# A six-layer transformer stretch on one core: ScalarE writes the first attention's mask, and three stages get their first operands sooner

## What is computed

```python
scores = jnp.einsum('bqhe,bkhe->bhqk', Q, K) / np.sqrt(d_head).astype(np.float32)
scores = jnp.where(causal, jnp.float32(IGNORE), scores)
A = jax.nn.softmax(scores, axis=-1)
```

## Time and profile before, and how to read them

| | |
|---|---|
| three runs | 1570.81, 1572.22, 1576.1 us; median 1572.22 |
| the profiled execution | 1575.96 us, its span in the trace 1574.0 us |
| TensorE matmul busy | 1528.8 us, 97% |
| TensorE weight load busy | 1319.7 us, 84% |
| VectorE busy | 992.5 us, 63% |
| ScalarE busy | 692.1 us, 44% |
| GpSimd busy | 204.5 us, 13% |
| mean granted TensorE clock | 0.989 of full |

### The profile page before, as it was taken

How to read it: one execution, slowest core, us unless ns; L and a number is a source line. 1 busy time by engine, 2 the same in 40 slices (tenths; PEclk the granted TensorE clock), 3 DMA queues, 4 the chain that set the end, 5 groups by cost and what they waited for, 6 DMA issues and landing times.

```text
span 1574.0 us, 28636 instructions
## 1 busy us (share of the span) xinstructions
PE 1528.8 (97%) x11080; PEld 1319.7 (84%) x11080; DVE 992.5 (63%) x2131; ACT 692.1 (44%) x1812; POOL 204.5 (13%) x215
## 2 busy tenths in 40 slices
PE   7999999999999999999999899999988999999997
PEld 6888888789999999988888767777766989999996
DVE  6777777875454545575666567788876464454547
ACT  3544444532222222223233267788875444444443
POOL 1322222310000000011000024121221300000001
PEclk9999999999999999999999989999999999999999
DMA  6000000001010101000000466678850000000101
GB/s 216 1 2 15 8 35 1 28 27 39 27 40 27 52 27 39 23 11 34 1 34 1 53 102 86 87 101 127 111 89 28 1 27 28 28 27 17 36 0 53
DMA packets 43082, 66.51 MB, mean 42 GB/s; under 512 B 4577, under 2 KB 33505, under 8 KB 42849
## 3 DMA queue, kind: packets, MB, share of 16 engines
q1 hardware_dynamic: 42976, 65.09, 20.3%
HBM read 36.24 MB, written 2.10 MB: 24 GB/s over the span
## 4 chain that ended last, share of the span: by engine, by line
PE 90%; DVE 5%; ACT 1%; DMA 1%; issue 1%; SPq 1%; POOL 0%; DVEq 0%; POOLq 0%; ACTq 0%
PE ps L85 24%; PE ps L86 23%; PE ps L87 22%; PE ps L1823 3%; PE ps L1837 2%; PE ps L392 2%; PE ps L403 2%; PE ps L416 2%; PE ps L1813 2%; PE ps L1868 2%; PE ps L1851 1%; PE ps L1810 1%; DMA nQs<-nQc_h 1%; PE ps L384 1%; SPq L1648 1%
## 5 line engine op out<-in xcount | busy, mean ns | idle before, releaser
L843 ACT ACTIVATE m2hT_h<-ps 128x512 fp32r<-128x512 f32 x128 | 76.7, 599 | 281.4 <-PE ps L87 281.4
L967 DVE TENSOR_TENSOR m6hT_l<-m6h,m6hT_h 128x512 fp32r<-128x512 f32 x128 | 88.6, 692 | 169.8 <-ACT m6hT_h L841 169.8
L969 DVE SCALAR_TENSOR_TENSOR m2hT_l<-ps,m2hT_h 128x512 fp32r<-128x512 f32 x128 | 88.5, 691 | 163.4 <-ACT m2hT_h L843 163.4
L840 ACT ACTIVATE m6h<-ps,m6b 128x512 f32<-128x512 f32 x128 | 88.2, 689 | 197.7 <-PE ps L87 193.8
L1949 ACT ACTIVATE nPr<-ps,negm 128x128 f32<-128x128 f32 x512 | 147.2, 384 | 27.3 <-DVE negm L2050 26.8
L87 PE MATMUL ps<-w_h,m6hT_l 128*128 128x256 f32 x512 | 144.4, 282 | 0.0
L85 PE MATMUL ps<-w_h,m6hT_h 128*128 128x256 f32 x512 | 143.5, 280 | 0.6 <-DVE m6hT_l L967 0.6
L86 PE MATMUL ps<-w_l,m6hT_h 128*128 128x256 f32 x512 | 143.7, 281 | 0.0
L87 PE MATMUL ps<-m2w_h,m2hT_l 128*128 128x256 f32 x448 | 126.8, 283 | 0.0
L86 PE MATMUL ps<-m2w_l,m2hT_h 128*128 128x256 f32 x448 | 126.7, 283 | 0.0
L85 PE MATMUL ps<-m2w_h,m2hT_h 128*128 128x256 f32 x448 | 126.3, 282 | 0.0
(11 more groups left out here) (318 smaller groups left out, 4327.2 us busy)
## 6 DMA issues: line engine op xcount, KB each, us to landing
nKm<-nKc_h SPq DMA_DIRECT2D x64, 128.0 KB, 4.3
nQs<-nQc_h SPq DMA_DIRECT2D x64, 128.0 KB, 5.9
raw<-in_w_e1i SPq DMA_DIRECT2D x9, 512.0 KB, 3.2
raw<-in_w_e1o SPq DMA_DIRECT2D x9, 512.0 KB, 3.2
raw<-in_w_e6i SPq DMA_DIRECT2D x9, 512.0 KB, 3.4
raw<-in_w_e6o SPq DMA_DIRECT2D x9, 512.0 KB, 3.3
nKm<-nKc_l SPq DMA_DIRECT2D x32, 128.0 KB, 4.8
nQs<-nQc_l SPq DMA_DIRECT2D x32, 128.0 KB, 5.9
```

Source lines behind the costliest of these rows:

```text
L840: nc.scalar.activation(c.h32[:, u % 2, :], ps[:, u % 2, :], ACT.Gelu, bias=bias)
L843: nc.scalar.activation(c.hT[0][:, ch, :], ps[:, u % 2, :], ACT.Relu).then_inc(c.s["hi_ready"], 1)
L967: last = nc.vector.tensor_tensor(c.hT[1][:, ch, :], c.h32[:, u % 2, :], c.hT[0][:, ch, :].bitcast(F32), ALU.subtract)
L969: last = nc.vector.scalar_tensor_tensor(c.hT[1][:, ch, :], ps[:, u % 2, :], 0.0, c.hT[0][:, ch, :].bitcast(F32), ALU.max, ALU.subtract)
```

## The change

ScalarE copies the bf16 mask from SBUF into each score bank when the exponentials of that bank are done (semaphore `masked`), for steps 1 to 31; the mask matmuls stay in step 0 alone, and Q K is added to the bank with `start=False`. In the first mixture the two x transposes of the routed stage stand ahead of `down(-2)`, and DVE does their low halves before group 2's normalisation and the last combine, which move behind the router's logits. In the last group of the routed stage x stands at chunk 6, the keys around `up(8)`, the queries after chunk 9's spread and `down(7)`. The last residual is done between the value copies, its statistics at n = 2 and its normalisation at n = 4; POOL's `residual(0)` waits for that. The keys of group 0 lie in `raw`, so layer 5's weights are loaded by `load_e6`, after the key layouts of group 0 have been read. The last mixture's x of group 0 has a place of its own (in wA5, dead by then), so only the third x waits for the layouts; its items are at other quads.

```diff
@@ scores (tensor)
-            if p > 0:
-                pe.wait_ge(s["p_exp"], 2 * p)
-            for half in range(2):
-                nc.tensor.matmul(ps[:, WSB[half], :], identb[:, :], causal[:, :, :].rearrange("p a b -> p (a b)"),
-                                 start=True, stop=False)
+                for half in range(2):
+                    nc.tensor.matmul(ps[:, WSB[half], :], identb[:, :], causal[:, :, :].rearrange("p a b -> p (a b)"),
+                                     start=True, stop=False)
+            else:
+                pe.wait_ge(s["masked"], 2 * p)
...
-                                            W.KT[G % 2][rows64, 4 * u + i, tok], start=False, stop=i == QH - 1)
+                                            W.KT[G % 2][rows64, 4 * u + i, tok], start=False, stop=p > 0 or i == QH - 1,
+                                            skip_group_check=p > 0)
@@ w_scalar
+        def mask(half):
+
+            nc.scalar.activation(ps[:, WSB[half], :], causal[:, :, :].rearrange("p a b -> p (a b)"),
+                                 ACT.Identity).then_inc(s["masked"], 1)
...
                     exponentials(2 * p + half)
+                if p < NP - 1:
+                    act.wait_ge(s["p_exp"], 2 * p + half + 1)
+                    mask(half)
@@ mix_setup
-        c.XT = pair(m, tag + "XT", [P, NG, DC, GT])
+        own = pair(m, tag + "XT", [P, NG, DC, GT])
+        c.XT = [[x[:, g, :, :] for g in range(NG)] for x in own]
...
+            for x, x0 in zip(c.XT, pair(Region(nc, a5_at, 8 * KB), tag + "XT0", [P, DC, GT])):
+                x[0] = x0[:, :, :]
@@ mix_tensor_parts
-                pe.wait_ge(N.s["z_ready"], NSEQS - GB)
-            if c.gelu and k == 4:
+                pe.wait_ge(N.s["z_ready"], NSEQS - GB - 1)
+            if c.gelu and k == 2:
+                pe.wait_ge(c.s["lt_taken"], 1)
+            elif c.gelu and k == 4:
...
-            pe.wait_ge(c.s["g_evac"], max(g + 1, 2) * DC + 2)
+            pe.wait_ge(c.s["g_evac"], (g + 1) * DC + 2)
@@ mix_tensor
-        down(i, -2)
         if between:
             between()
+        down(i, -2)
         down(i, -1, halves=c.gelu)
@@ mix_vector
                 if between and u == NU - 1:
                     between(0)
-                normalise(q - NG)
+                    between(1)
+                else:
+                    normalise(q - NG)
             weights(i, u)
         if not c.gelu:
-            between(1)
-            combine(i, 2 * NG - 1)
+            def last_combine():
+                normalise(NG - 2)
+                combine(E_OUT // 2 - 1, 2 * NG - 1)
@@ ffn_order
-                early = [("x", k) for k in range(DC)] if last and c == FC - DC else []
-                order += early[:1] + [("u", c)] + early[1:] + ([("s", c)] if c >= SC else []) + [("t", c)]
-            if c == FC - 1 and last:
-                order.append(("nk", 0))
+                x = [("x", k) for k in range(DC)] if last and c == FC - 4 else []
+                k = [("nk", k) for k in range(DC)] if last and c == FC - 2 else []
+                order += x[:1] + k[:1] + ([("nk evac", 0)] if k else []) + [("u", c)] + x[1:] + k[1:]
+                order += ([("s", c)] if c >= SC else []) + ([("nq", 0)] if last and c == FC - 1 else []) + [("t", c)]
...
-                order += [("h", c - 1), ("nk", 1), ("nq", 0), ("d", c - 2), ("nq", 1)]
+                order += [("nq evac", 0), ("nq", 1), ("h", c - 1), ("nq evac", 1), ("d", c - 2)]
...
+            if c == FC - 2 and last:
+                order.append(("nk evac", 1))
@@ ffn_vector
                 elif kind == "l":
                     logits(g)
+                    if type(g) is int and g == 0:
+                        of_mixture[0]()
@@ n_order_vector, n_following
-            order += n_fill_of(n - 1) + [f for f in later if f not in shared] + ([("fn", 0)] if n == 1 else [])
+            order += n_fill_of(n - 1) + [f for f in later if f not in shared] + ([("fs", 0)] if n == 2 else []) + ([("fn", 0)] if n == 4 else [])
...
-    M_X_AT, M_L_AT, M_U_AT, M_D_AT = (6, 7, 8, 9, 14, 15), (10, 11, 16), (16, 17, 18, 19), (20, 21)
-    M_B_AT, M_G_AT, M_E_AT = (12,), (12, 13, 17), 16
+    M_X_AT, M_L_AT, M_U_AT, M_D_AT = (2, 4, 7, 9, 15, 16), (6, 11, 17), (16, 17, 18, 19), (20, 21)
+    M_B_AT, M_G_AT, M_E_AT = (13,), (13, 14, 17), 17
@@ n_pool, residual
-                pool.wait_ge(F3.s["x_done"], (g + 1) * GB)
+                pool.wait_ge(F3.s["x_done"], B if g == 0 else (g + 1) * GB)
@@ n_scalar
             elif kind == "mx":
-                if i == 0:
+                if i == DC:
@@ n_vector
-                if i == (0, GB - 1):
-                    of_ffn[0]()
+                if i[0] == 0:
+                    of_ffn[0](i[1])
+            elif kind == "fs":
+                of_ffn[1]()
             elif kind == "fn":
-                of_ffn[1]()
+                of_ffn[2]()
@@ sync
-            for k in range(2):
-                load_unit(sp, U_A5, k, w_a5[:, k * 768:(k + 1) * 768], 768)
...
             def load_e6():
                 sp.wait_ge(stage_done, 3)
+                for j in range(2):
+                    sp.wait_ge(N.k_laid[j], LAID)
+                    sp.sem_inc(waited_sp, 1)
+                for k in range(2):
+                    load_unit(sp, U_A5, k, w_a5[:, k * 768:(k + 1) * 768], 768)
```

More of the change, by code:

```diff
@@ L757, in logits @@
             rows_hl, rows_h = ps[0:2 * E_OUT, 5, :], ps[0:E_OUT, 5, :]
-            nc.tensor.matmul(rows_hl, both[0], c.XT[0][:, g, 0, :], start=True, stop=False)
+            nc.tensor.matmul(rows_hl, both[0], c.XT[0][g][:, 0, :], start=True, stop=False)
             for i in range(DC):
-                nc.tensor.matmul(rows_h, gw[:, i, 0, :], c.XT[1][:, g, i, :], start=False, stop=False)
-            nc.tensor.matmul(rows_hl, both[1], c.XT[0][:, g, 1, :], start=False, stop=True).then_inc(c.s["logits"], 1)
+                nc.tensor.matmul(rows_h, gw[:, i, 0, :], c.XT[1][g][:, i, :], start=False, stop=False)
+            nc.tensor.matmul(rows_hl, both[1], c.XT[0][g][:, 1, :], start=False, stop=True).then_inc(c.s["logits"], 1)
         def logits_back(half):
@@ L1197, in ffn_x @@
     def ffn_x(g, ch):
-        return (FX - DC if ffn_last(g) else FX) + ch
+        return (FX - 4 if ffn_last(g) else FX) + ch
     def ffn_spread(g, c):
-        return c + (DC if ffn_last(g) and c >= FC - DC else 0)
+        return c + (DC if ffn_last(g) and c >= FC - 4 else 0)
     def ffn_sync(sp):
@@ L1274, in spread @@
             bank = g_fill(g, ffn_spread(g, c))
+            if ffn_last(g) and c >= FC - 2:
+                pe.wait_ge(N.s["g_evac"], n_filled(0, NK + c - (FC - 2)))
             if c == SC:
@@ L1436, in gates_transposed, with sums_of, residual_of @@
             nc.vector.tensor_tensor(lo, src, hi.bitcast(F32), ALU.subtract).then_inc(s["g_evac"], 1)
+        def sums_of(g):
+            return f_last if ffn_last(g) else F3.r
+        def residual_of(g, j):
+            acc = ps[:, 6 + j // 2, (j % 2) * D:(j % 2 + 1) * D]
+            nc.vector.tensor_tensor(sums_of(g)[:, j, :], acc, X[:, g * GB + j, :], ALU.add).then_inc(s["r_done"], 1)
         def residual(g):
@@ L1470, in steps @@
                         following()
-                elif kind in ("nk", "nq"):
+                elif kind in ("nk evac", "nq evac"):
                     n_lo_qk(v, 0, kind[1], c)
@@ L1479, in steps @@
                     if type(g) is int and g == 0:
-                        of_mixture[0]()
+                        of_mixture[1]()
                 elif kind == "t":
@@ L1503, in ffn_vector, with last_residual @@
         ffn_groups(v, steps)
-        def last_stats():
-            residual(NG - 1)
-            norm_stats(NG - 1)
-            v.sem_inc(stage_done, 1)
-        return last_stats, lambda: norm(NG - 1)
+        def last_residual(j):
+            if j == 0:
+                v.wait_ge(s["d_full"], NG)
+            residual_of(NG - 1, j)
+            if j == GB - 1:
+                v.wait_ge(s["r_done"], NG * GB + C1)
+                v.sem_inc(stage_done, 1)
+        return last_residual, lambda: norm_stats(NG - 1), lambda: norm(NG - 1)
     NGG = 2 * NG
@@ L1537, in program @@
     N.XT0 = pair(Region(nc, m.at, 8 * KB), "nXT0", [P, DC, GT])
-    N.Kc0 = pair(Region(nc, r1.start + 8 * FU * 4, 8 * KB), "nKc0", [P, DC, GT])
+    N.Kc0 = pair(Region(nc, keep.start + B * D * 4, 8 * KB), "nKc0", [P, DC, GT])
+    f_last = Region(nc, r1.start + 8 * FU * 4, 4 * KB).place("f3last", [P, GB, D], F32)
     N.Pr = m.place("nPr", [P, 4, QH, S], F32)
@@ L1620, in n_following @@
         return order + ([("mu", M_U_AT.index(k - later))] if k - later in M_U_AT else [])
-    n_ring = [f for f in n_order() if f[0] in ("x", "k", "q", "v") or f[0] == "zb" and f[1] < NSEQS - GB]
+    n_ring = [f for f in n_order() if f[0] in ("x", "k", "q", "v") or f[0] == "zb" and f[1] < NSEQS - GB - 1]
     n_place = {f: F for F, f in enumerate(n_ring)}
@@ L2195, in split_e6 @@
```

(4 more changed lines are left out.)

24 lines of the change are left out of this document (12 added, 12 removed).

## The result

The changed kernel takes 1560.39 us (median of four, 1556.92 to 1562.81); the kernel before, on the same chip, 1571.97 (1570.81 to 1576.1). The ratio is 0.9926, 95% interval 0.9911 to 0.994: faster by 11.6 us. The forecast was 27.6 faster, 1544.6, range 1537 to 1557. The sign was right and the size was not.

What follows compares the result with a forecast made beforehand. TensorE was taken to bound the kernel, at 90% of the chain and fully busy in the first attention. Terms 13.0 - 0.2 + 7.3 + 7.5 = 27.6 us, from 1572.2, gave 1544.6 us, range 1537 to 1557.

Steps and rivals of the forecast that it cites:

- A: First attention: ScalarE writes the mask and 62 of 64 mask matmuls go; 13.0 us gained, between 8 and 15.
- B: First mixture's end: TensorE's 1.61 us wait for x goes, but VectorE's list still ends last; 0.2 us lost.
- C: Start of the heads-of-16 run: earlier layouts and shorter stalls, less a new wait at quad 16; 7.3 us gained.
- D: Last mixture's head: fewer waits for x and logits and less half clock; 7.5 us gained, between 3 and 8.5.
- the 0.50 for each pair: First attention: time saved per removed pair of mask matmuls, in us; 31 pairs give 15.5.
- the fourth rival: First attention: Q K pays the switch the mask paid, 0.43 us per pair, 2.2 less gained; 1547 us, chance 0.08.
- the last lands near 937: Before quad 16: group 1's twelve layouts issue from 922.2 at 1.03 us each; quad 16 waits 2.8 us.
- the prediction's signs: List of what would show it right; here, scores of quad 0 at 5 us less wait.
- of which 4 would come back: Quad 0 to quad 16: of some 9 us of half-clock stretches, 4 us would be regained.
- one of about 1 us remains: Last mixture's head: of four waits for x, 3.9 us, one stays, between the fifth and sixth x.
- That leaves 4.4: Last mixture's head: us won from waits for x and logits after the two that stay.
- The third rival: Seams stall anew: C and D give half, 7.4 instead of 14.8 us; 1552 us, chance 0.17.

Runs made afterwards that it cites:

- five kernels: Five kernels that differ elsewhere but keep the changed kernel's load order at quad 16; TensorE waits there were 3.76, 3.70, 3.47, 1.46 and 0.40 us.
- the second execution of the kernel before: The unchanged kernel before, executed and profiled once more: 1570.57 us, against 1575.96 us in the profiled execution the forecast rests on.

## Why the prediction was right and wrong

The forecast's mechanisms were right in A and B. Its steps that failed are the time at which the layouts land in C and, in D, the count of waits that would go, which left out the waits that came instead.

**A, 13.0 forecast, 10.9 in its stage.** The term that was mis-sized is the 0.50 for each pair: 0.43 was measured, since the rest stands before Q K as before. That was the fourth rival, which had a chance of 0.08; it is 31 x 0.07 = 2.2 less. The short steps' cover held: 0.05 us were left at the values, and the 0.6 charged for them was not due. Steps 1 and 2 cost 0.8 and not 0.5; steps 30 and 31 fell 2.5 behind the other steps' gain, not 1.4. 31 x 0.43 less these is 10.0. The other 0.9 is luck: the first Q K starts 0.8 us sooner in this profile (23.50, and 24.31 before), ahead of the first step that the change touches, since TensorE's first 256-column matmuls run at 0.41 us until 12.2 and not 14.3; this start also differs by 0.4 us between the two profiles of the kernel before. Mask rows of 0.60 were as forecast. The Trainium skill's lower latency in PSUM (ScalarE: Activation LUTs, "Step-by-step: what each stage is for") is hardly to be seen: of copies that read SBUF, 0.60 to PSUM (from bf16) and 0.62 to SBUF (from fp32).

**B, 0.2 lost forecast, 0.2 lost measured**, with the 1.61 wait turned into 1.56 and 1.94 for VectorE's gates and product. The mechanism is shown by the run with the part undone; that the number is met to 0.1 us is luck, as profiles of one kernel differ by more.

**C, 7.3 forecast, 2.4 in the profiles.** The mechanism was right: TensorE waits at quad 16 for layouts behind the splits and the loads. The step that failed is the time put on it: "the last lands near 937". By the old clock (10.65 us added) they landed at 940.8. The normalisation at quad 4 ended at 911.7, not at about 910, and GpSimd's residual behind it, so the layouts issued at 924.5 and not 922.2; and from there to the start of quad 16 it took 16.2 us and not 14.8. The sum had no term for the loads ahead of them in the queue, nor for the scatter of 3 us that five kernels show there. Behind the wait came 1.5 us from a slow stretch, where 0.5 was charged. That is 4.8 of the 4.9. Two errors stay hidden behind this wait: quad 0 gained 3.2 and not 3.9 (its wait is 3.1 shorter, where the prediction's signs said 5), and of the slow stretches "of which 4 would come back" the second execution of the kernel before had most back without the change. They show where the wait is gone: quad 0 to quad 16 then takes 36.0, where 34.6 was forecast.

**D, 7.5 forecast, 0.2 in the profiles.** The step that failed is "one of about 1 us remains", and with it "That leaves 4.4". For x 2.0 us remain. The longest wait for logits does stay, 1.5 as forecast, so waits for x and logits lost 3.4 in all. But only the waits named in the rows were followed, and not what else moves: gates, their exponentials and the last logits are one step later too, on a VectorE where x stands behind them. The wait for the hidden units grew from 0.66 to 1.86, three new ones of 0.79 to 0.88 came for `z` and the probabilities, and the head's waits sum to 6.3 where they were 6.5. The 2.9 for half-clock windows was not won: the changed kernel's profile has two such stretches in the head as well. Nor was all of it the waits' own, since the second profile of the kernel before has the same waits and neither stretch.

**The sum.** Forecast 27.6; measured by profiles 13.2, by medians 11.6. The difference by profiles, 14.4, is A 2.1, C 4.9 and D 7.3. The third rival (the seams stall anew) was nearest, and it took half of C and D where nearly all went (2.6 of 14.8 are left).

## What to carry to other kernels

Price a matmul that is removed by doubling it or by what stands before its successor: of the 0.53 us from this pair to the next instruction only 0.43 went with it. A stretch at half clock behind a short stall can be there in one execution and not in the next: take a second profile before its microseconds are counted as something to win. When steps are moved, follow every list that they stand in up to the point where the stage ends: here one queue's loads (4.3 us) and one step of a hand-written order (2.9 us) decided more than the waits that were removed.

## What was not expected of the hardware

- Two executions of one kernel with the same stalls had 34 and 16 us of their spans at half clock, and took 1575.96 and 1570.57 us.
- One 128 KB transfer out of twelve landed 3.3 us after the one before it in one kernel and 1.2 us in another, with the same transfers ahead of it, and TensorE waited for it.
- A first attention that ended 1.1 us sooner went with 4.9 us over the whole kernel, by the ratios. The cause was not found.
- Thirteen stalls of 0.2 us, one every 18 us, cost just their sum, 2.8 us, and no clock.
